# A decoder layer's cross-attention: VectorE forms the cosine term of the rotation alone, ScalarE copies the exchanged halves, GpSimd multiplies them with the sines and adds

## What is computed

```
q = (query @ Wq).reshape(nb, q_len, H, D).transpose(0, 2, 1, 3)
k = (key @ Wk).reshape(nb, q_len, KVH, D).transpose(0, 2, 1, 3)
q = q * cos + _rotate_half(q) * sin          # _rotate_half(x) = concat([-x2, x1])
k = k * cos + _rotate_half(k) * sin
scores = jnp.einsum('bhqd,bhkd->bhqk', q, k) / sqrt(D)   # k, v repeated over groups of 4 heads
scores = where(mask == 0, -1e9, scores); attn = softmax(scores)
x = (attn @ v), heads joined, @ Wo
```

## Time and profile before

| | |
|---|---|
| time, median of 3 runs | 1413.53 us (1412.81 to 1415.68) |
| the profiled execution's own time | 1413.3 us |
| its span | 1411.1 us |
| TensorE busy | 1379.6 us, 98% of the span |
| VectorE busy | 1021.5 us, 72% |
| ScalarE busy | 440.7 us, 31% |
| GpSimd busy | 529.2 us, 37% |
| VectorE's three rotation instructions in cross-attention | 128 times each |

### The profile page before, as it was taken

One profiled execution on the slowest core, in us unless ns is written; L12 is line 12 of the kernel. 1 busy time (PEld: TensorE's weight loads), 2 busy tenths in 40 slices (PEclk: granted clock), 3 DMA queues, 4 the chain that ended last, 5 costly groups with the idle time before them and its releaser, 6 DMA issues.

```text
span 1411.1 us, 27857 instructions
## 1 busy us (share of the span) xinstructions
PE 1379.6 (98%) x11552; PEld 1146.4 (81%) x11552; DVE 1021.5 (72%) x1476; ACT 440.7 (31%) x751; POOL 529.2 (37%) x457
## 2 busy tenths in 40 slices
PE   8999999999997799999999999999999999999999
PEld 6888888788886688888888888888888888888787
DVE  3755553788989977767767767777777777778765
ACT  5311233666657442122122122113123122122432
POOL 4422310444344524344344344344344344342131
PEclk9999999999999999999999999999999999999999
DMA  8654220000005012012011012011011011002011
GB/s 268 218 180 148 99 89 1 18 3 25 10 3 166 16 34 73 16 46 61 16 46 60 16 46 60 16 46 54 22 46 48 28 46 46 31 16 89 30 53 67
DMA packets 78859, 83.03 MB, mean 59 GB/s; under 512 B 9824, under 2 KB 50928, under 8 KB 78480
## 3 DMA queue, kind: packets, MB, share of 16 engines
q1 hardware_dynamic: 68832, 63.16, 14.3%
q10 hardware_dynamic: 9360, 17.04, 3.9%
q0 software_dynamic: 544, 1.06, 0.3%
HBM read 58.17 MB, written 23.07 MB: 58 GB/s over the span
## 4 chain that ended last, share of the span: by engine, by line
PE 60%; POOL 3%; DVE 1%; ACT 0%; issue 0%; ACTq 0%
PE p_ps_y L1272 6%; PE p_ps_y L1273 6%; PE p_ps_y L1274 6%; PE p_ps_qk L75 4%; PE p_ps_s L1233 3%; PE p_ps_qk L77 3%; PE p_ps_qk L76 3%; POOL p_wo_lo L1196 3%; PE p_ps_s L1244 2%; PE p_ps_s L1272 2%; PE p_ps_s L1274 2%; PE p_ps_s L1273 2%; PE p_ps_o L76 2%; PE p_ps_o L75 2%; PE p_ps_s L75 2%; PE p_ps_o L77 2%
## 5 line engine op out<-in xcount | busy, mean ns | idle before, releaser
L1650 POOL TENSOR_TENSOR p_q_rot<-p_q_rot,p_rb 128x512 f32<-128x512 f32 x128 | 167.2, 1306 | 310.7 <-DVE p_rb L171 310.7
L1272 PE MATMUL p_ps_y<-p_wo_hi,p_o_hi 128*128 128x512 f32 x384 | 151.2, 394 | 2.0 <-DVE p_o_lo L1526 1.3
L1273 PE MATMUL p_ps_y<-p_wo_lo,p_o_hi 128*128 128x512 f32 x384 | 149.5, 389 | 0.0
L1274 PE MATMUL p_ps_y<-p_wo_hi,p_o_lo 128*128 128x512 f32 x384 | 149.4, 389 | 0.0
L75 PE MATMUL p_ps_qk<-p_xt_hi,p_wq_hi 128*128 128x512 f32 x312 | 126.8, 406 | 0.9 <-DVE p_xt_lo L1550 0.9
L1031 POOL TENSOR_TENSOR p_pn<-p_p,p_inv 128x512 f32<-128x512 f32 x64 | 66.1, 1063 | 154.2 <-DVE p_inv L920 152.0
L1535 DVE TENSOR_TENSOR x_sb<-p_ps_y,x_sb 128x512 f32<-128x512 f32 x96 | 66.4, 692 | 77.0 <-PE p_ps_y L1274 76.0
L77 PE MATMUL p_ps_qk<-p_xt_hi,p_wq_lo 128*128 128x512 f32 x312 | 122.0, 391 | 0.0
L76 PE MATMUL p_ps_qk<-p_xt_lo,p_wq_hi 128*128 128x512 f32 x312 | 121.8, 390 | 0.0
L1380 ACT ACTIVATE p_pt_hi<-p_ps_s 128x512 fp32r<-128x512 f32 x64 | 34.9, 597 | 257.8 <-PE p_ps_s L1244 257.7
L1386 ACT ACTIVATE p_o_hi<-p_ps_s 128x512 fp32r<-128x512 f32 x64 | 34.7, 595 | 230.0 <-PE p_ps_s L1259 230.0
(11 more groups left out here) (262 smaller groups left out, 3774.1 us busy)
## 6 DMA issues: line engine op xcount, KB each, us to landing
k_scratch<-p_k_out SPq DMA_DIRECT2D x32, 256.0 KB, 2.1
p_raw<-in_wq SPq DMA_DIRECT2D x32, 256.0 KB, 3.2
p_raw<-in_wo SPq DMA_DIRECT2D x32, 256.0 KB, 2.7
p_k_t<-k_scratch ACTq DMA_DIRECT2D x32, 256.0 KB, 2.7
p_v_in<-v_scratch ACTq DMA_DIRECT2D x32, 256.0 KB, 2.8
v_scratch<-p_v_out SPq DMA_DIRECT2D x24, 256.0 KB, 2.6
x_sb<-in_x SPq DMA_DIRECT2D x16, 256.0 KB, 3.0
out<-p_y SPq DMA_DIRECT2D x16, 256.0 KB, 2.0
```

The costliest lines, as they stand in the source:

```text
L1272: nc.tensor.matmul(ps_y[t][:, :], oh, w_hi["o"][h][:, :], start=(h == 0), stop=False)
L1273: nc.tensor.matmul(ps_y[t][:, :], oh, w_lo["o"][h][:, :], start=False, stop=False)
L1274: mm = nc.tensor.matmul(ps_y[t][:, :], ol, w_hi["o"][h][:, :], start=False, stop=(h == H - 1))
L1650: nc.gpsimd.tensor_tensor(q_rot[:, h, :], q_rot[:, h, :], rb[:, :], ALU.add).then_inc(q_added, 1)
```

## The change

The rotation of the queries in cross-attention is spread over three engines. The keys' rotation in the first stage stays as it is.

- VectorE's `rotate(it, h)` does only the cosine product. It no longer waits for the sum of the head before.
- ScalarE gets a new function `exchange(it, h)`: two copies of 64 partitions each, from the upper half of the PSUM bank to the lower half of `rb` and the other way. It waits for `q_terms` of its head and for the sum of the head before, and counts on a new semaphore `q_moved`.
- GpSimd's `add_terms` first multiplies `rb` by the sines in place, waits for that, and then adds. `q_added` now counts two for each head.
- The sine table is loaded with its halves exchanged, in two DMAs of 64 partitions in place of one DMA.
- TensorE's waits for a free bank ask for `q_moved` as well as `q_terms`. `projections_over` waits for the last sum too.
- A semaphore (`negated`) is merged into another (`folded`), to stay in their number.

The places of `exchange` in ScalarE's order are in the diff.

```diff
--- before.py
+++ after.py
@@ -856,7 +856,7 @@
                 spread_q(it + 1)
                 if b == NB - 2 and g + 1 < G1:
                     split_hi(act, "q", g + 1, done["q"], it + 2)
-            cross_normalise, cross_hi, cross_weights, cross_loads, rest = cross.scalar(act)
+            cross_normalise, cross_hi, cross_weights, cross_loads, cross_exchange, rest = cross.scalar(act)
             outputs_hi(ITS - 3)
             norm2.finish_scalar(nc, act, 0)
             move_values(ITS - 1)
@@ -884,16 +884,21 @@
             cross_weights(0, 2)
             cross_weights(0, 3)
             cross_loads()
+            cross_exchange(0, 0)
             outputs_hi(ITS - 1)
             norm2.finish_scalar(nc, act, 2)
+            cross_exchange(0, 1)
             cross_hi(4)
             cross_normalise(6)
             cross_hi(5)
             cross_normalise(7)
+            cross_exchange(0, 2)
             cross_hi(6)
             cross_normalise(8)
             cross_hi(7)
             cross_normalise(9)
+            cross_exchange(0, 3)
+            cross_exchange(1, 0)
             rest()
 
         @block.vector
@@ -1113,11 +1118,11 @@
 
         mask_in, masked, tables_in = m.sem("mask_in"), m.sem("masked"), m.sem("tables_in")
         xn_ready, transposed, all_hi, all_lo = (m.sem(n) for n in ("xn_ready", "transposed", "all_hi", "all_lo"))
-        negated, folded = m.sem("negated"), m.sem("folded")
+        folded = m.sem("folded")
         raw_in = [m.sem(f"raw_in{h}") for h in range(H)]
         part_hi, ready = {w: m.sem(f"part_hi_{w}") for w in "qo"}, {w: m.sem(f"ready_{w}") for w in "qo"}
         k_in, v_loaded, v_part, v_ready = (m.sem(n) for n in ("k_in", "v_loaded", "v_part", "v_ready"))
-        q_done, q_terms, q_added = m.sem("q_done"), m.sem("q_terms"), m.sem("q_added")
+        q_done, q_moved, q_terms, q_added = m.sem("q_done"), m.sem("q_moved"), m.sem("q_terms"), m.sem("q_added")
         s_done, s_bound, s_max, s_shifted = m.sem("s_done"), m.sem("s_bound"), m.sem("s_max"), m.sem("s_shifted")
         p_exp, p_sum, p_inv, p_norm, p_turned = (m.sem(n) for n in ("p_exp", "p_sum", "p_inv", "p_norm", "p_turned"))
         pt_part, pt_ready = m.sem("pt_part"), m.sem("pt_ready")
@@ -1127,6 +1132,7 @@
 
             engine.wait_ge(q_done, ITS * H)
             engine.wait_ge(q_terms, ITS * H)
+            engine.wait_ge(q_added, 2 * ITS * H)
 
         lin = LoraLinear(nc, m, base, ([ps_free_q, ps_o[0]], [ps_free_q, ps_s[1]], ps_s, ps_free_q, [ps_o[0], ps_o[2]]),
                          projections_over, x, norm3, ident, linear_drams)
@@ -1157,7 +1163,8 @@
             need(sp, prior["v_placed"], PRIOR_ITS)
             need(sp, prior["v_moved"], PRIOR_ITS)
             sp.dma_start(cos_t[:, :], cos_scr).then_inc(tables_in, 16)
-            sp.dma_start(sin_t[:, :], sin_scr).then_inc(tables_in, 16)
+            for r in range(2):
+                sp.dma_start(sin_t[r * HALF:(r + 1) * HALF, :], sin_scr[(1 - r) * HALF:(2 - r) * HALF, :]).then_inc(tables_in, 16)
             need(sp, prior["s_done"], PRIOR_ITS)
             for r in range(2):
                 sp.dma_start(bound[r * SEQ:(r + 1) * SEQ, :, :].bitcast(I32), mask_dram).then_inc(mask_in, 16)
@@ -1207,12 +1214,14 @@
                     need(pe, prior["out_lo"], PRIOR_ITS)
                 need(pe, ready["q"], 4 * (it // NB) + h + 1)
                 if h == 0:
-                    need(pe, q_terms, (it - 1) * H + 3)
+                    read = (it - 1) * H + 3
                 elif h == 2:
-                    need(pe, q_terms, it * H + 1)
+                    read = it * H + 1
                 else:
+                    read = (it - 1) * H + h + 1
                     need(pe, out_lo, 2 * (it - 2) + h // 2 + 1)
-                    need(pe, q_terms, (it - 1) * H + h + 1)
+                need(pe, q_terms, read)
+                need(pe, q_moved, read)
                 product3(nc, ps_q[h][:, :], [(w_hi["q"][h][:, c * P:(c + 1) * P], w_lo["q"][h][:, c * P:(c + 1) * P],
                                               xt_hi[:, c, tokens(it)], xt_lo[:, c, tokens(it)]) for c in range(KC)]).then_inc(q_done, 1)
 
@@ -1220,7 +1229,7 @@
 
                 if it >= ITS:
                     return
-                need(pe, q_added, (it + 1) * H)
+                need(pe, q_added, 2 * (it + 1) * H)
                 if it == 2:
                     need(pe, all_lo, TILES)
                 need(pe, k_in, (it + 1) * 16)
@@ -1250,6 +1259,7 @@
                 need(pe, pt_ready, 2 * it + half + 1)
                 need(pe, all_lo, 3 * TPB)
                 need(pe, q_terms, min((it + 1) * H + 2 * half + 2, ITS * H))
+                need(pe, q_moved, min((it + 1) * H + 2 * half + 2, ITS * H))
                 need(pe, y_added, (it - 1) * TPB + half + 2)
                 for t in range(half * UT, (half + 1) * UT):
                     tile = slice(t * P, (t + 1) * P)
@@ -1365,6 +1375,20 @@
                 need(act, v_ready, it)
                 act.dma_start(v_in[:, :], v_scr[it // NB, it % NB, :, :, :].rearrange("p t d -> p (t d)")).then_inc(v_loaded, 16)
 
+            def exchange(it, h):
+
+                if it >= ITS:
+                    return
+                k = it * H + h
+                need(act, q_terms, k + 1)
+                need(act, q_added, 2 * k)
+                if k == 0:
+                    need(act, prior["v_placed"], PRIOR_ITS)
+                    need(act, prior["v_moved"], PRIOR_ITS)
+                for r in range(2):
+                    c = nc.scalar.activation(rb[r * HALF:(r + 1) * HALF, :], ps_q[h][(1 - r) * HALF:(2 - r) * HALF, :], ACT.Copy)
+                c.then_inc(q_moved, 1)
+
             def values_hi(it):
                 need(act, v_loaded, (it + 1) * 16)
                 need(act, pv_done, it * 2)
@@ -1387,7 +1411,7 @@
                                          ps_o[2 * half + r][:, :].rearrange("p (t h q) -> p t h q", t=UT, h=H), ACT.Copy).then_inc(out_hi, 1)
 
             def normalise_tile(t):
-                need(act, folded, t // TPB + 1)
+                need(act, folded, 2 * (t // TPB + 1))
                 need(act, transposed, t - 1)
                 if t >= 3 * TPB:
                     need(act, ready["o"], t % 2 + 1)
@@ -1415,14 +1439,17 @@
                 load_values(1)
                 tile_parts_hi(8)
                 normalise_tile(10)
+                exchange(1, 1)
                 tile_parts_hi(9)
                 normalise_tile(11)
+                exchange(1, 2)
                 tile_parts_hi(10)
                 need(act, prior["y_done"], PRIOR_ITS * TPB)
                 turned_hi(0, 0)
                 tile_parts_hi(11)
                 turned_hi(0, 1)
                 norm2.finish_scalar(nc, act, 3)
+                exchange(1, 3)
                 normalise_tile(12)
                 normalise_tile(13)
                 for it in range(LAST - 1):
@@ -1434,11 +1461,14 @@
                     outputs_hi(it, 1)
                     values_hi(it + 1)
                     exponentials(it + 1)
+                    exchange(it + 2, 0)
                     load_keys(it + 2)
                     load_values(it + 2)
                     if b == 1 and g + 1 < KVH:
                         split_q_hi(act, g + 1, 0)
                         split_q_hi(act, g + 1, 1)
+                    exchange(it + 2, 1)
+                    exchange(it + 2, 2)
                     turned_hi(it + 1, 0)
                     turned_hi(it + 1, 1)
                     if it == 0:
@@ -1451,6 +1481,7 @@
                     if b == 1 and g + 1 < KVH:
                         split_q_hi(act, g + 1, 2)
                         split_q_hi(act, g + 1, 3)
+                    exchange(it + 2, 3)
                 outputs_hi(LAST - 1, 0)
                 outputs_hi(LAST - 1, 1)
                 values_hi(LAST)
@@ -1473,7 +1504,7 @@
                     lin.tile_parts_hi(act, n)
                     lin.rank_parts_hi(act, n)
 
-            return normalise_tile, tile_parts_hi, lambda g, h: split_q_hi(act, g, h), first_loads, rest
+            return normalise_tile, tile_parts_hi, lambda g, h: split_q_hi(act, g, h), first_loads, exchange, rest
 
         def vector(dve):
             def shift(it):
@@ -1506,14 +1537,13 @@
                     return
                 k = it * H + h
                 need(dve, q_done, k + 1)
-                need(dve, q_added, k)
                 need(dve, s_done, it)
                 if k == 0:
-                    need(dve, tables_in, 32)
+                    need(dve, tables_in, 48)
                     need(dve, prior["p_norm"], PRIOR_ITS * 4)
                 if k == 2:
                     need(dve, prior["pv_done"], PRIOR_ITS)
-                rotate_terms(nc, ps_q[h], cos_t[:, tokens(it)], sin_t[:, tokens(it)], q_rot[:, h, :], rb).then_inc(q_terms, 1)
+                nc.vector.tensor_tensor(q_rot[:, h, :], ps_q[h][:, :], cos_t[:, tokens(it)], ALU.mult).then_inc(q_terms, 1)
 
```

(12 more changed lines are left out.)

## The result

The kernel after took 1424.28 us (median of 4 runs, 1423.53 to 1425.96), the kernel before 1413.46 (median of 4 beside it, 1412.81 to 1415.68). The ratio is 1.0075, 95% interval 1.0058 to 1.0093: slower by 10.8 us. The forecast was 1419.8 us in a range of 1415.5 to 1427: sign and range held, the size was 4.5 us short. The upper end that the forecast's own sum gives, 1423.9, was passed by 0.4 us; the time lies in the stated range because that reached further.

What follows compares the result with a forecast made beforehand. TensorE was taken to bound cross-attention, with waits where it starts. Lateness of 3.6 us up to scores(1) plus 2.7 in body 0, 6.3 us, on the profiled 1413.3 gave 1419.6, plus 0.2 for the median: 1419.8; range 1415.5 to 1427.

Steps and rivals of the forecast that it cites:

- Step 1: First iterations, scores(0): GpSimd's product is slowed beside VectorE's mask instructions; start at 474.2 us instead of 473.23.
- Step 2: ScalarE's exchange(1, 0) waits for scores(0) ahead of the output weights; GpSimd's low parts start at 479.3, 6.2 us late.
- Step 3: GpSimd's work from the low parts to turn(0, 0), which starts at 493.9 us instead of 490.90: 3.0 late.
- Step 4: From turn(0, 0) to scores(1), which start at 502.3 us instead of 498.70: 3.6 late in all.
- Body 0: exchange(2, 3) stands behind the high parts of tiles 14 and 15; scores(2) start a further 2.7 us late.
- Ordinary bodies and the end: Later loop bodies and the linear layer's loads: slack (2.4 us, 1.7 with b = 1) hides the change; cost 0.
- the first rival: Clock stays low past 502.3 us, so scores(1) and the projections behind take longer: +3 us, 1422.8; chance 0.12.
- The rival of waiting ordinary bodies: Loop bodies wait for GpSimd, four operations taking 2.31 us instead of 1.29: 1437 or 1471 us; chance 0.10.

Runs made afterwards that it cites:

- e6: Kernel after, with needless 512-column matmuls added where TensorE waits, and three waits to protect banks still read: 1421.75 us, ratio 1.0053 to the kernel before.
- e2: Kernel after, with exchange(2, 3) in body 0 moved ahead of the high parts of tiles 14 and 15: 1421.85 us, ratio 1.0048 to the kernel before.
- e1: Kernel after, with exchange(1, 0) moved behind the split of the output weights on ScalarE: 1421.63 us, ratio 1.0052 to the kernel before.

## Why the prediction was right, and where its size was off

- **Step 1, scores(0), held.** Product beside VectorE's mask instructions 2.22 us (2.31 was taken), start late by 1.0 as forecast.
- **Step 2, the wait that hurts, held.** ScalarE reached the output weights' split only after scores(0); the low parts started 0.3 us later behind the end of scores(0) than worked out (3.3 instead of 3.0). They start at 481.81 and not near 479, because scores(0) also start later and take longer.
- **Step 3, 2.0 between scores(0) and turn(0, 0), came out as 2.7** beside the longer scores: 0.3 from step 2, 0.1 from the low parts (6.13 instead of 6.0), and 0.3 from exchange, product, sum and scaling of head (1, 1), which end 4.95 us behind head (1, 0) instead of 4.7. Two things sit in that: an exchange takes 1.20 us, not 1.1 (that price was read from whole-bank copies), and from product to sum it is 1.33 to 1.37 us from start to start where instructions without a wait between them take 1.25.
- **Step 4, 0.6 from turn(0, 0) to scores(1), came out as 1.6.** In e6, at full clock, the leg is 8.45 us against 7.80 before: 0.65, the forecast. The other 0.9 is gone at full clock.
- **Body 0, 2.7, came out as 3.1.** exchange(2, 3) starts where it was forecast, behind the high parts, and from its start to the end of the sum it is 3.9 us (535.32 to 539.22) instead of 3.6. TensorE idles 1.25 us ahead of mix(1, 1) and 1.53 ahead of scores(2). For the first the profile names an addition on VectorE, but the code needs only the third addition of iteration 0 there, done at 531.25, and exchange(2, 3), done at 536.51, which reads the bank that mix(1, 1) writes. e2 shows that it is the exchange: with it earlier both waits are gone, and the same mixing starts ahead of that addition. The kernel after, and then e2:

```profile
535.32 1.19 ACT L1389 ACTIVATE p_rb<-p_ps_o 64x512 f32<-64x512 f32 x2
536.05 0.68 DVE L1565 TENSOR_TENSOR x_sb<-p_ps_y,x_sb 128x512 f32<-128x512 f32 x1
```

```profile
535.97 0.28 PE L1269 MATMUL p_ps_o<-p_pt_hi,p_v_hi 64*128 64x256 f32 x1
...
536.66 0.68 DVE L1567 TENSOR_TENSOR x_sb<-p_ps_y,x_sb 128x512 f32<-128x512 f32 x1
```

- **Ordinary bodies and the end, 0, held** (+0.1). TensorE is busy 784.4 of 788 us between 510 and 1298. A body with b = 1, the tightest kind, kept 0.9 us of slack, not 1.7. Its last sum and its scores:

```profile
989.62 1.29 POOL L1686 TENSOR_TENSOR p_q_rot<-p_q_rot,p_rb 128x512 f32<-128x512 f32 x1
...
991.79 2.08 PE L1242 MATMUL p_ps_s<-p_k_t,p_q_rot 128*64 128x64 f32 x64
```

- **The term that was missing: the clock was priced at 0 in the sum.** It is the first rival, given 0.12 and 3 us (scores(1) and the projections behind them; a low clock under scores(0) it did not have). It happened, beside the forecast and not instead of it, with 3.7 us by e6's trace up to scores(2). The argument against it was that in the kernel before scores(1) took 2.09 us behind mixing products that also ran after a wait. But step 3 of the same sum made the wait before turn(0, 0) longer (3.62 to 5.04 us), and step 1 put a wait of about 2 us (2.27 measured) ahead of scores(0), where there had been 0.50: both waits follow from the forecast's own numbers and were not carried to the clock. The 4.9 us between 6.3 forecast and 11.2 in the trace are these 3.7 and 1.2 us of small terms. The waits, their places and their order were right by reasoning. That the time still fell into the range was due to the range's width.

The rival of waiting ordinary bodies asked for GpSimd operations at 2.31 in the loop; their means are 1.29 and 1.30. In the passage the slow ones stand beside two kinds of VectorE instruction: the product of 471.53 (2.22 us) beside the second mask instruction (471.40, an addition with one input, from SBUF to SBUF), and in e1 the sum of 481.68 (2.17 us) beside the subtraction of the maxima at 480.79, two inputs from SBUF:

```profile
480.79 1.90 DVE L1525 TENSOR_TENSOR p_s<-p_s,p_mx 128x1024 f32<-128x1024 f32 x1
```

VectorE pays there too: 1.90 us, where the same line takes 1.22 in the kernel after at 481.80. There GpSimd was busy as well, but had started its low parts 0.01 us later, and it paid: 6.13 us for the four, 4.98 in e1. In e1 the subtraction started 0.46 us behind the product of 480.33. In these rows the one that started second lost the time. The Trainium skill ("GPSIMD Engine Reference", Key points) names these two kinds, instructions in a two-port mode or with two SBUF inputs, as those that GpSimd contends with; the rows agree, as far as the mask instruction is of the first kind. No row says so, but it passes 2048 elements a partition in 1.23 us, and the subtraction with two inputs 1024 in 1.22.

## What to carry to other kernels

On an engine that runs its instructions in order, a new instruction costs not what it takes but what it waits for, if work that is ready stands behind it: 1.2 us of copies cost 3 us in one place, and the same copies cost nothing in the loop, where every order had slack. Unloading an engine that nobody waits for (176 us here) buys nothing; look first at whether the bottleneck waits for it, stage by stage. When the profile names a releaser, check it against the code's waits: two of the waits here were put down to the wrong engine. And when a sum of waits makes TensorE idle longer or in a new place, price the work behind each of these waits at the low clock, as a term and not as a rival.
